# Attention maximum over two key halves: formed by GpSimd as difference, positive part and sum, with constant rows of -1

## The chip, the cores and the metric

The kernel runs on one core of a Trainium2 chip. The metric is the device time of one execution in microseconds; for a kernel, the median over its runs.

## What is computed

The program computes two layers over an input of 2 x 2048 tokens of width 128: `x = x + s * g`, where `s` comes from one branch and `g = silu(...)` from another. The first layer's `s` is the part that the change touches. Its two attention blocks have 8 heads of width 8 each, which gives 16 heads for each of the two batch rows:

```
q = (xin @ wq.T + bq).reshape(b, s, H, DK)      # H = 8, DK = 8
k = (xin @ wk.T + bk).reshape(b, s, H, DK)
scores = einsum('bshd,bthd->bhst', q, k) * (1.0 / sqrt(DK))
a = softmax(scores, axis=-1)
o = einsum('bhst,bthd->bshd', a, v)
```

The softmax subtracts the largest score of each query before the exponential. Beside it stands a mixture of 32 experts (4 for each token, at most 640 tokens for each expert), and behind both a state-space scan with a second, per-sequence expert network.

## The kernel before, in words

The program is written engine by engine, with semaphores between the engines and a fixed order on each. The attention is cut into 32 **units** (`UNITS`, one head of one batch row each). A unit has 2048 queries and 2048 keys.

For each unit there are two passes of TensorE over the scores:

- The **maximum pass** has 32 chunks (`CHUNKS`). Chunk n takes 128 queries against one half of the keys, 1024 of them, as two bf16 matmuls into two PSUM banks (`max_scores`, L1950). VectorE reduces each 128 x 1024 chunk to one column of `mxp` (L897): `mxp[:, n // 2, n % 2]` holds the maximum over key half n % 2 of query tile n // 2. There are two pairs of banks, so TensorE may be two chunks ahead of VectorE (the wait on `mx_done` in `max_scores`).
- The **score pass** has 64 steps e (`EXPS`). Each is one 512-column matmul (L2063), whose result ScalarE turns into exponentials (L1312). Groups of four exponentials are multiplied with the values (`weigh`, L1966). Twice in a unit ScalarE also evacuates the accumulated output (`evac`, L1301).

TensorE interleaves them: after every second score step comes one maximum chunk of a later place. The chunks run ahead by somewhat more than half a unit, so that chunk 0 of a unit is issued at about step 13 of the unit before, chunk 16 at about step 45, and chunk 31 at about step 11 of the unit itself.

Once 16 chunks (half a unit, 8 query tiles) are reduced, the maximum travels this way:

1. VectorE, `negated` (L849 to L854): one `tensor_reduce` of the 128 x 8 x 2 block of `mxp` to 128 x 8 with `negate=True`, into `nmx[:, 0]`. On VectorE's queue it stands behind the first chunk of the next half. It waits also for `spl_ready`, that is until GpSimd is done with an earlier half.
2. GpSimd, `largest` (L1602 to L1610): it waits for `nmx_ready` and splits the number in three bf16 parts with four small instructions (L1607 to L1610, a `plink` wait on the engine's own semaphore between them), into `spl`.
3. SyncE, `load_max` (L532 to L541): a DMA transpose of `spl` into `mT` (L537), and then two DMAs (L541) that put the three parts as rows into the query stacks `QS`. They raise `m_ld`.
4. TensorE's score pass waits for `m_ld` at steps 0 and 32 of each unit (L2060). The key stacks `KS` have constant rows at the same place. They are set once by GpSimd (L1578) and copied to the other stacks by SyncE; with rows of 1 in the keys and the negated maximum in the queries, the matmul L2063 yields score minus maximum.

The maximum pass uses 48 rows of the stacks (`MAXROWS`), the score pass 51, so that only the latter sees the constant rows.

GpSimd does other work in its fixed order between the calls of `largest`. In the first units it makes the routing tables of the experts (`plain` with `rows_step`). In the units called 12 to 19 there (`scatter`) it issues 16 indirect DMAs a unit (L1629), each released by one `pv_done` of TensorE; `largest(u - 3, 1)` stands ahead of the fourth and `largest(u - 2, 0)` ahead of the twelfth. Because of the offset of three, these run while TensorE is in the score pass of units 9 to 16. After the expert stage (785 to 910 us, in which no chunk is in work) it issues 12 indirect gathers a unit (`gather`, L1659), with `largest(u - 3, 1)` ahead of the fourth and `largest(u - 2, 0)` behind the last, followed by a `combine` of the unit before (L1637 to L1646). These run beside the score pass of units 18 to 28.

Of the kernel before, what the change touches and what calls it, by code (L numbers as in the profile page):

```python
# [6 lines left out]
ALU = mybir.AluOpType  # L7
# [3 lines left out]
X_AX = mybir.AxisListType.X  # L11
# [10 lines left out]
UNITS = G * B  # L22
# [9 lines left out]
TCH = S // P  # L32
STEPS = 2 * TCH
DFF = 512
CHUNKS = 2 * TCH
# [85 lines left out]
def after(eng, sem, count):  # L121

    if not isinstance(count, int) or count > 0:
        eng.wait_ge(sem, count)


def build(nc, a, out):
# [3 lines left out]
    with ExitStack() as ctx:  # L131
        def sb(name, shape, dt=F32):
            return ctx.enter_context(nc.sbuf_tensor(name, shape, dt))

        def sem(name):
            return ctx.enter_context(nc.semaphore(name))

        def dram(name, shape, dt=F32):
# [67 lines left out]
        KS = [stacks[:, (4 + i) * S:(5 + i) * S] for i in range(4)]  # L206
# [85 lines left out]
        mxp = sb("mxp", [P, TCH, 2])  # L292
        nmx = sb("nmx", [P, 2, TCH])
# [18 lines left out]
        ones_set = sem("ones_set")  # L312
# [16 lines left out]
        vh_ready, mxs_ready, mx_done, spl_ready, mt_ld = (  # L329
            sem(n) for n in ("vh_ready", "mxs_ready", "mx_done", "spl_ready", "mt_ld"))  # L330
# [12 lines left out]
        nmx_ready = sem("nmx_ready")  # L343
# [405 lines left out]
        def _(v):  # L749
# [72 lines left out]
            for d in range(1, NG):  # L822
                first, second = slice(0, NG - d), slice(d, NG)
# [22 lines left out]
            ins.then_inc(part2k, 1)  # L846


            def negated(uu, half):  # L849
                tiles = slice(TCH // 2 * half, TCH // 2 * (half + 1))  # L850
                v.wait_ge(mx_done, CHUNKS * uu + CHUNKS // 2 * (half + 1))
                after(v, spl_ready, 2 * uu + half - 1)
                v.tensor_reduce(nmx[:, 0, tiles], mxp[:, tiles, :], X_AX, ALU.max, negate=True).then_inc(nmx_ready, 1)  # L853

            def expert_h(e, w):
                v.wait_ge(sg_done, e + 1)
                v.wait_ge(mh_ready, 2 * e + 2)
                after(v, mo_ready, e - 1)
                halves = lambda t: t.rearrange("p (h c) -> p h c", h=2)
                v.tensor_tensor(halves(hhe[w % 2]), halves(sge[w % 2]), PS[:, 4:6, 0:CAP // 2], ALU.mult).then_inc(hh_done, 1)  # L860

            def expert_out(e, w, uses):
                v.wait_ge(mo_ready, e + 1)
                after(v, oes_st[w % 2], 16 * uses)
                v.tensor_copy(oe_s[w % 2][:, 0:512], PS[:, 6, :])
                v.tensor_copy(oe_s[w % 2][:, 512:CAP], PTF[:, 0:CAP - 512]).then_inc(oe_out, 1)  # L866
# [14 lines left out]
            def expert_stage():  # L881
                for e in range(E):
                    expert_h(e, e % 4)
                    if e > 0:
                        expert_out(e - 1, (e - 1) % 4, (e - 1) // 2)
                    if 0 <= e - NB - 2 < 4:
                        sums_inverse(0, e - NB - 2)
                    if e == NB + 6:
                        sum_weights()
                expert_out(E - 1, 3, E // 2 - 1)  # L890

            for uu in range(UNITS):
                for n in range(CHUNKS):
                    if CHUNKS * uu + n == CHUNK_AT:
                        expert_stage()
                    v.wait_ge(mxs_ready, CHUNKS * uu + n + 1)
                    v.tensor_reduce(mxp[:, n // 2, n % 2:n % 2 + 1], MXB[n % 2].rearrange("p a c -> p (a c)"), X_AX, ALU.max).then_inc(mx_done, 1)  # L897
                    if n == 0 and uu > 0:
                        negated(uu - 1, 1)
                    if n == CHUNKS // 2:  # L900
                        negated(uu, 0)
            negated(UNITS - 1, 1)


            v.wait_ge(c_ld, 16 * NLATE)
# [22 lines left out]
            half = lambda j: lambda t: PS[:, RES_BANK[j], t * DH:(t + 1) * DH]  # L928
# [192 lines left out]
            with v.If(v.value_load(flag[:, :], min_val=0, max_val=1) > 0):  # L1121
# [20 lines left out]
                for half in range(2):  # L1142
                    v.wait_ge(g_st, 16 * B * S // GT + 32 + 16 * half)
                    tiles = slice(NT // 2 * half, NT // 2 * (half + 1))
# [429 lines left out]
        def _(pool):  # L1574
            for i in range(4):
                pool.memset(VH[i][:, :, :], 1.0).then_inc(ones_set, 1)
            pool.wait_ge(ones_set, 4)
            pool.memset(KS[0][32:64, :], 1.0).then_inc(ones_set, 1)  # L1578
            pool.wait_ge(ones_set, 5)
            pool.memset(zt[:, :], 0.0).then_inc(ones_set, 1)  # L1580
            pool.wait_ge(ones_set, 6)
# [18 lines left out]
            plink = Chain(pool, pool_chain).link  # L1600

            def largest(uu, half):  # L1602
                tiles = slice(TCH // 2 * half, TCH // 2 * (half + 1))
                first, second = nmx[:, 0, tiles], nmx[:, 1, tiles]
                pool.wait_ge(nmx_ready, 2 * uu + half + 1)
                after(pool, mt_ld, 16 * (2 * uu + half - 1))
                plink(pool.tensor_copy(spl[:, half, 0, :], first))  # L1607
                plink(pool.tensor_tensor(second, first, spl[:, half, 0, :], ALU.subtract))
                plink(pool.tensor_copy(spl[:, half, 1, :], second))
                pool.tensor_tensor(spl[:, half, 2, :], second, spl[:, half, 1, :], ALU.subtract).then_inc(spl_ready, 1)  # L1610
# [840 lines left out]
```

## Time and profile before

| what | value |
|---|---|
| median of 3 runs | 1840.53 us (1836.5 to 1842.19) |
| the profiled execution | 1841.78 us |
| its span in the profile | 1839.7 us |
| mean granted TensorE clock | 0.974 of full speed |
| PE busy | 1711.9 us, 93% of the span |
| DVE (VectorE) busy | 1617.7 us, 88% |
| ACT (ScalarE) busy | 1477.5 us, 80% |
| POOL (GpSimd) busy | 654.0 us, 36% |
| HBM traffic | 74 GB/s over the span |

The span is what the profiler sees between the first and the last instruction; the execution's own time is 2.1 us more, and its time lies 1.25 us above the median of the runs. Busy times are shares of one engine's span and do not add up. Instructions of one engine may overlap in the records: the next one can start some tens of nanoseconds before the last one's end, so the time from start to start, not the mean duration, tells an engine's rate. The attention runs from about 77 us to 1432 us, with the expert stage in its middle.

### The profile page before, as it was taken

Reading aid. Unit: us, or ns where it says so; the run is one execution under the profiler, and the core shown is the slowest. Engines: PE = TensorE matmul, PEld = TensorE weight load, DVE = VectorE, ACT = ScalarE, POOL = GpSimd, SP = SyncE. Lnnn points to the kernel's source line nnn. Section 1 sums busy time; section 2 is a strip of 40 time slices with the busy share of each in tenths; the row PEclk is TensorE's granted clock in tenths of the full one; section 3 lists DMA queues with packets and bytes.
Section 4 is the critical chain, followed back from the end, with each engine's and each line's share of the span. In section 5 each row is a group of like instructions: output and inputs, shape, how many; then the busy total and the mean of one; then the engine's idle time right before and its main releaser. Section 6 shows DMA issues by size and latency. Waiting matters only on the chain.

```text
span 1839.7 us, 40114 instructions
## 1 busy us (share of the span) xinstructions
PE 1711.9 (93%) x15395; PEld 667.3 (36%) x15396; DVE 1617.7 (88%) x2338; ACT 1477.5 (80%) x2809; POOL 654.0 (36%) x932
## 2 busy tenths in 40 slices
PE   6799999999999999999999999999999699799784
PEld 4332222222222222278622222222222244366553
DVE  7799999999999999945599999999996677599778
ACT  5569999999999998943499999999999557777455
POOL 1423210232444444100045655566401233133447
PEclk9899999999999999999999999999999899899897
DMA  4422122111221122278412111211103233422121
GB/s 125 164 74 87 58 85 68 62 55 36 66 66 55 57 62 65 74 207 227 137 50 64 53 48 49 64 54 47 38 11 81 80 117 92 130 70 54 38 73 46
DMA packets 151357, 142.15 MB, mean 77 GB/s; under 512 B 38986, under 2 KB 130125, under 8 KB 151010
## 3 DMA queue, kind: packets, MB, share of 16 engines
q1 hardware_dynamic: 142818, 122.36, 22.6%
q0 software_dynamic: 8352, 17.29, 3.3%
q8 instruction: 118, 1.93, 0.5%
q14 instruction: 69, 0.57, 0.1%
HBM read 76.60 MB, written 60.03 MB: 74 GB/s over the span
## 4 chain that ended last, share of the span: by engine, by line
PE 72%; DVE 12%; ACT 9%; issue 4%; DMA 1%; POOL 1%; SPq 0%; DVEq 0%; ACTq 0%; POOLq 0%
PE PS L1966 28%; PE PS L2063 18%; PE PS L1950 10%; ACT probs L1312 7%; PE PS L2013 4%; PE PS L1998 2%; DVE hst L1084 1%; DVE VP L1061 1%; PE PS L1990 1%; PE PS L2176 1%; PE PS L2319 1%; DVE waq L919 1%; PE PS L2113 1%; DVE VP L1069 1%; DVE MXV L1090 1%
## 5 line engine op out<-in xcount | busy, mean ns | idle before, releaser
L897 DVE TENSOR_REDUCE mxp<-PS 128x1 f32<-128x1024 f32 x1024 | 1172.7, 1217 | 30.0 <-PE PS L1950 25.4
L1312 ACT ACTIVATE probs<-PS 128x512 f32<-128x512 f32 x2048 | 1096.2, 597 | 71.0 <-PE PS L2063 27.4
L1966 PE MATMUL PS<-probs,VH 128*32 128x256 f32 x8192 | 642.5, 391 | 2.3 <-ACT probs L1312 1.0
L2063 PE MATMUL PS<-stacks 51*128 51x512 bf16 x2048 | 444.0, 388 | 22.7 <-ACT probs L1312 18.7
L1950 PE MATMUL PS<-stacks 48*128 48x512 bf16 x2048 | 418.3, 381 | 9.6 <-DMA stacks<-qkl_d 8.5
L1966 PEld LDWEIGHTS PS<-probs,VH 128*32 128x32 f32 x8192 | 173.0, 108 | 400.1 <-issue 220.3
L2063 PEld LDWEIGHTS PS<-stacks 51*128 51x128 bf16 x2048 | 116.2, 93 | 463.7 <-ACT probs L1312 380.6
L1659 POOL DMA_INDIRECT S<-oe_d,ROWI x128 | 130.2, 1017 | 132.5 <-PE PS L1966 125.3
L1629 POOL DMA_INDIRECT xe_d<-S,ROWI x128 | 125.1, 977 | 140.1 <-PE PS L1966 118.0
L1607 POOL CAST spl<-nmx 128x8 bf16<-128x8 f32 x64 | 12.7, 199 | 305.7 <-DVE nmx L853 227.5
L1950 PEld LDWEIGHTS PS<-stacks 48*128 48x128 bf16 x2048 | 105.3, 95 | 34.0 <-DVE mxp L897 12.3
L1615 POOL TENSOR_TENSOR VH<-VP,bvb 128x128 f32<-128x128 f32 x32 | 14.4, 451 | 233.3 <-DMA oe_d<-XNT 138.3
L860 DVE TENSOR_TENSOR probs<-probs,PS 128x640 f32<-128x640 f32 x32 | 26.3, 821 | 58.0 <-ACT probs L1346 52.2
L2013 PE MATMUL PS<-probs,ews 128*128 128x320 f32 x256 | 74.3, 433 | 0.2 <-ACT probs L1346 0.2
L1337 ACT ACTIVATE probs<-PS 128x640 f32<-128x640 f32 x32 | 22.6, 705 | 61.4 <-PE PS L1990 61.3
L1810 POOL TENSOR_TENSOR stacks<-stacks,VH 128x512 f32<-128x512 f32 x16 | 24.9, 1555 | 92.7 <-ACT stacks L1497 92.7
L2013 PEld LDWEIGHTS PS<-probs,ews 128*128 128x128 f32 x256 | 46.1, 190 | 15.6 <-issue 0.4
L1998 PEld LDWEIGHTS PS<-ews,probs 128*128 128x128 f32 x320 | 40.7, 192 | 6.1 <-issue 1.2
L1998 PE MATMUL PS<-ews,probs 128*128 128x128 f32 x320 | 41.0, 275 | 1.1 <-DVE XNT L866 1.1
L1301 ACT ACTIVATE SG<-PS 128x512 f32<-128x512 f32 x64 | 37.9, 592 | 2.4 <-PE PS L1966 2.4
L1481 ACT ACTIVATE VP<-PS 128x1024 f32<-128x1024 f32 x16 | 16.4, 1025 | 26.2 <-PE PS L2243 24.7
L2176 PE MATMUL PS<-stacks,probs 128*128 128x512 f32 x64 | 33.4, 648 | 2.7 <-ACT SG L1413 2.7
(360 smaller groups left out, 1863.7 us busy)
## 6 DMA issues: line engine op xcount, KB each, us to landing
stacks<-qkl_d SPq DMA_DIRECT2D x128, 96.0 KB
xe_d<-zt SPq DMA_DIRECT2D x16, 640.0 KB
XNT<-xe_d SPq DMA_DIRECT2D x32, 320.0 KB, 3.8
oe_d<-XNT SPq DMA_DIRECT2D x32, 320.0 KB, 3.2
stacks<-qkl_d SPq DMA_DIRECT2D x128, 64.0 KB
o_d<-SG SPq DMA_DIRECT2D x256, 32.0 KB
ews<-in_ew_dram SPq DMA_DIRECT2D x33, 192.0 KB, 2.4
stacks<-qkl_d SPq DMA_DIRECT2D x128, 32.0 KB
```

Of the source, the lines that this page charges most:

```text
L860: v.tensor_tensor(halves(hhe[w % 2]), halves(sge[w % 2]), PS[:, 4:6, 0:CAP // 2], ALU.mult).then_inc(hh_done, 1)
L897: v.tensor_reduce(mxp[:, n // 2, n % 2:n % 2 + 1], MXB[n % 2].rearrange("p a c -> p (a c)"), X_AX, ALU.max).then_inc(mx_done, 1)
L1301: act.activation(OE[half][:, :], OB, ACT.Copy).then_inc(o_evac, 1)
L1312: act.activation(probs[:, at:at + 512], PS[:, bank_of(u, e), :], ACT.Exp, scale=float(1.0 / np.sqrt(np.float32(DK)))).then_inc(exp_done, 1)
L1629: pool.indirect_dma_start(xe_d, bass.IndirectOffsetOnAxis(ROWI[:, t, n:n + 1], 0), S0[:, t, :], None, bounds_check=E * CAP - 1, oob_is_err ...
L1659: pool.indirect_dma_start(GB[:, t % (2 * TB), n, :], None, oe_d, bass.IndirectOffsetOnAxis(ROWI[:, t, n:n + 1], 0), bounds_check=last_row, ...
L1950: mm = pe.matmul(MXB[n % 2][:, i, :], QS[w][o:o + MAXROWS, (n // 2) * P:(n // 2 + 1) * P], KS[w][o:o + MAXROWS, key:key + 512], start=True ...
L1966: mm = pe.matmul(OB[32 * jg:32 * jg + 32, c:c + 256], VH[w][:, kt, :], probs[:, at:at + 256], start=(kt < 2 and half == 0), stop=(kt >= TC ...
L1998: mm = pe.matmul(o, hhe[w % 2][:, t * P:(t + 1) * P], EW[w][:, 2, :], start=True, stop=True)
L2013: mm = pe.matmul(PS[:, 2 + 2 * m + h, 0:CAP // 2], EW[w][:, m, :], xeT[w % 2][:, h * CAP // 2:(h + 1) * CAP // 2], start=True, stop=True)
L2063: pe.matmul(PS[:, bank_of(u, e), :], KS[w][o:o + KROWS + 3, kt * P:(kt + 1) * P], QS[w][o:o + KROWS + 3, q0:q0 + 512], start=True, stop=Tr ...
L2176: pe.matmul(PS[:, 5 - t % 2, :], PJ[j][:, cols(t)], win[:, 0:2 * DI], start=True, stop=True).then_inc(zx_ready, 1)
```

## The change

On VectorE the function `negated` goes, with its 64 calls. The wait on `spl_ready` that stood in it moves to the first chunk of each half: VectorE may not overwrite half of `mxp` before GpSimd has read the earlier unit's values there. On GpSimd, `largest` waits for the 16 chunks themselves (`mx_done`) and forms the maximum of the two key halves a and b as `a + max(b - a, 0)`, with three instructions ahead of its four. The result is no longer negated, and the constant rows of the keys become -1 in its place. The order on TensorE, ScalarE and SyncE stays as it was.

```diff
@@ VectorE
-            def negated(uu, half):
-                tiles = slice(TCH // 2 * half, TCH // 2 * (half + 1))
-                v.wait_ge(mx_done, CHUNKS * uu + CHUNKS // 2 * (half + 1))
-                after(v, spl_ready, 2 * uu + half - 1)
-                v.tensor_reduce(nmx[:, 0, tiles], mxp[:, tiles, :], X_AX, ALU.max, negate=True).then_inc(nmx_ready, 1)
...
                 for n in range(CHUNKS):
                     if CHUNKS * uu + n == CHUNK_AT:
                         expert_stage()
+                    if n % (CHUNKS // 2) == 0:
+                        after(v, spl_ready, 2 * uu + n // (CHUNKS // 2) - 1)
                     v.wait_ge(mxs_ready, CHUNKS * uu + n + 1)
                     v.tensor_reduce(mxp[:, n // 2, n % 2:n % 2 + 1], MXB[n % 2].rearrange("p a c -> p (a c)"), X_AX, ALU.max).then_inc(mx_done, 1)
-                    if n == 0 and uu > 0:
-                        negated(uu - 1, 1)
-                    if n == CHUNKS // 2:
-                        negated(uu, 0)
-            negated(UNITS - 1, 1)
@@ GpSimd
-            pool.memset(KS[0][32:64, :], 1.0).then_inc(ones_set, 1)
+            pool.memset(KS[0][32:64, :], -1.0).then_inc(ones_set, 1)
...
             def largest(uu, half):
                 tiles = slice(TCH // 2 * half, TCH // 2 * (half + 1))
                 first, second = nmx[:, 0, tiles], nmx[:, 1, tiles]
-                pool.wait_ge(nmx_ready, 2 * uu + half + 1)
+                of_keys = [mxp[:, tiles, i] for i in range(2)]
+                pool.wait_ge(mx_done, CHUNKS * uu + CHUNKS // 2 * (half + 1))
+                plink(pool.tensor_tensor(second, of_keys[1], of_keys[0], ALU.subtract))
+                plink(pool.tensor_scalar(second, second, 0.0, None, ALU.max))
+                plink(pool.tensor_tensor(first, of_keys[0], second, ALU.add))
                 after(pool, mt_ld, 16 * (2 * uu + half - 1))
                 plink(pool.tensor_copy(spl[:, half, 0, :], first))
```

GpSimd's queue at the first unit of the scatter stage, before (L1629 is an indirect DMA, the bracket names the semaphores that a row waits for):

```order
L1629 DMA xe_d<-S,ROWI 20480x128
L1629 DMA xe_d<-S,ROWI 20480x128 [waits pv_done] x2
L1607 CAST spl<-nmx 128x8 [waits mt_ld,nmx_ready,pv_done]
L1608 TENSOR_TENSOR nmx<-nmx,spl 128x8 [waits pool_chain]
L1609 CAST spl<-nmx 128x8 [waits pool_chain]
L1610 TENSOR_TENSOR spl<-nmx,spl 128x8 [waits pool_chain]
L1629 DMA xe_d<-S,ROWI 20480x128
L1629 DMA xe_d<-S,ROWI 20480x128 [waits pv_done] x7
```

The same place in the changed kernel (lines 1598 to 1605 are its `largest`, line 1624 the indirect DMA):

```order
L1624 DMA xe_d<-S,ROWI 20480x128
L1624 DMA xe_d<-S,ROWI 20480x128 [waits pv_done] x2
L1598 TENSOR_TENSOR nmx<-mxp 128x8 [waits mx_done,pv_done]
L1599 TENSOR_SCALAR nmx<-nmx 128x8 [waits pool_chain]
L1600 TENSOR_TENSOR nmx<-mxp,nmx 128x8 [waits pool_chain]
L1602 CAST spl<-nmx 128x8 [waits mt_ld,pool_chain]
L1603 TENSOR_TENSOR nmx<-nmx,spl 128x8 [waits pool_chain]
L1604 CAST spl<-nmx 128x8 [waits pool_chain]
L1605 TENSOR_TENSOR spl<-nmx,spl 128x8 [waits pool_chain]
L1624 DMA xe_d<-S,ROWI 20480x128
L1624 DMA xe_d<-S,ROWI 20480x128 [waits pv_done] x7
```

Three instructions, each waiting for the one before, now stand between the third and the fourth indirect DMA, and the wait for `nmx_ready` has become one for `mx_done`.

VectorE's queue at the start of the maximum pass, before:

```order
L897 TENSOR_REDUCE mxp<-PS 128x1 [waits mxs_ready] x17
L853 TENSOR_REDUCE nmx<-mxp 128x8 [waits mx_done]
L897 TENSOR_REDUCE mxp<-PS 128x1 [waits mxs_ready] x16
L853 TENSOR_REDUCE nmx<-mxp 128x8 [waits mx_done]
L897 TENSOR_REDUCE mxp<-PS 128x1 [waits mxs_ready] x16
L853 TENSOR_REDUCE nmx<-mxp 128x8 [waits spl_ready,mx_done]
```

and in the changed kernel (line 893 is the reduction of a chunk):

```order
L893 TENSOR_REDUCE mxp<-PS 128x1 [waits mxs_ready] x32
L893 TENSOR_REDUCE mxp<-PS 128x1 [waits mxs_ready,spl_ready]
L893 TENSOR_REDUCE mxp<-PS 128x1 [waits mxs_ready] x15
L893 TENSOR_REDUCE mxp<-PS 128x1 [waits mxs_ready,spl_ready]
L893 TENSOR_REDUCE mxp<-PS 128x1 [waits mxs_ready] x15
```

The small reductions are gone, and from the second unit on every 16th chunk has a second semaphore to wait for.

## Rows read from the trace of the kernel before

**Rows 1.** The page: busy us, share of the span and instructions of each engine.

```profile
PE 1711.9 (93%) x15395; PEld 667.3 (36%) x15396; DVE 1617.7 (88%) x2338; ACT 1477.5 (80%) x2809; POOL 654.0 (36%) x932
```

**Rows 2.** Groups by line: names, shapes, count | busy us, mean ns | idle us before, releaser.

```profile
L897 DVE TENSOR_REDUCE mxp<-PS 128x1 f32<-128x1024 f32 x1024 | 1172.7, 1217 | 30.0 <-PE PS L1950 25.4
L1608 POOL TENSOR_TENSOR nmx<-nmx,spl 128x8 f32<-128x8 f32 x64 | 13.2, 206 | 5.4
L1714 POOL TENSOR_SCALAR gs<-gs 128x32 f32<-128x32 f32 x1 | 0.3, 299 | 0.1
```

**Rows 3.** Waits over the whole span: us in total, times, longest us.

```profile
POOL spl L1607 <- DVE nmx L853: 227.5, 22, 19.4
...
PEld PS L1950 <- DVE mxp L897: 12.3, 21, 1.0
```

**Rows 4.** Windows, one unit each: length, then busy of PE, PEld, DVE, ACT, POOL.

```profile
372.72:409.45 36.73, 36.22 (x389) 9.58 (x386) 36.54 (x35) 35.06 (x67) 12.69 (x21) 1.00 0.22 69
...
594.64:631.60 36.96, 36.34 (x389) 10.66 (x386) 36.54 (x35) 35.17 (x67) 17.61 (x25) 1.00 0.20 61
...
1170.61:1207.48 36.87, 36.36 (x388) 9.65 (x385) 36.63 (x35) 34.98 (x67) 21.89 (x33) 1.00 0.20 54
```

**Rows 5.** Timeline of PE in unit 7: start us, length us, line.

```profile
378.72 0.39 PE L2063 MATMUL PS<-stacks 51*128 51x512 bf16 x2
...
383.18 0.41 PE L2063 MATMUL PS<-stacks 51*128 51x512 bf16 x2
```

**Rows 6.** Timeline of DVE in unit 8, merged runs of one line.

```profile
416.14 2.35 DVE L897 TENSOR_REDUCE mxp<-PS 128x1 f32<-128x1024 f32 x2
418.40 0.16 DVE L853 TENSOR_REDUCE nmx<-mxp 128x8 f32<-128x16 f32 x1
418.47 14.89 DVE L897 TENSOR_REDUCE mxp<-PS 128x1 f32<-128x1024 f32 x13
433.67 1.23 DVE L897 TENSOR_REDUCE mxp<-PS 128x1 f32<-128x1024 f32 x1 [0.30 <-PE PS L1950]
...
439.41 11.39 DVE L897 TENSOR_REDUCE mxp<-PS 128x1 f32<-128x1024 f32 x10
```

**Rows 7.** Timeline of POOL in unit 9 (scatter stage).

```profile
455.99 0.19 POOL L1607 CAST spl<-nmx 128x8 bf16<-128x8 f32 x1 [0.56 <-PE PS L1966]
456.27 0.20 POOL L1608 TENSOR_TENSOR nmx<-nmx,spl 128x8 f32<-128x8 f32 x1
...
457.50 1.02 POOL L1629 DMA_INDIRECT xe_d<-S,ROWI  x1 [0.50 <-issue]
458.94 0.97 POOL L1629 DMA_INDIRECT xe_d<-S,ROWI  x1 [0.42 <-issue]
461.18 0.97 POOL L1629 DMA_INDIRECT xe_d<-S,ROWI  x1 [1.27 <-PE PS L1966]
```

**Rows 8.** Timeline of DVE at the same place.

```profile
455.50 4.61 DVE L897 TENSOR_REDUCE mxp<-PS 128x1 f32<-128x1024 f32 x4
460.32 3.49 DVE L897 TENSOR_REDUCE mxp<-PS 128x1 f32<-128x1024 f32 x3 [0.21 <-PE PS L1950]
```

**Rows 9.** Timeline in unit 16, three indirect DMAs in a row: POOL's last, DVE behind it.

```profile
721.86 0.98 POOL L1629 DMA_INDIRECT xe_d<-S,ROWI  x1 [0.55 <-issue]
...
723.70 2.44 DVE L897 TENSOR_REDUCE mxp<-PS 128x1 f32<-128x1024 f32 x2 [0.57 <-PE PS L1950]
```

**Rows 10.** Timeline of POOL at the start of unit 26 (gather stage).

```profile
1209.90 0.46 POOL L1615 TENSOR_TENSOR VH<-VP,bvb 128x128 f32<-128x128 f32 x1 [1.08 <-PE PS L1966]
```

**Rows 11.** Timeline of SP and PE at the start of units 2 and 26.

```profile
184.09 1.54 SPq L541 DMA_DIRECT2D stacks<-mT  x2
...
186.88 0.39 PE L2063 MATMUL PS<-stacks 51*128 51x512 bf16 x2 [0.84 <-DMA stacks<-mT]
...
1203.31 1.56 SPq L541 DMA_DIRECT2D stacks<-mT  x2
...
1207.48 0.39 PE L2063 MATMUL PS<-stacks 51*128 51x512 bf16 x2
```

## The prediction

> **What bounds the kernel now.** The change touches the attention alone, so I asked who paces a unit there. The page [rows 1] does not say: TensorE, VectorE and ScalarE are all busy for 80% or more of the span, and GpSimd for 36%. Next I read the groups by line. VectorE's chunk reductions are the costliest group of the program, 1172.7 us for 1024, with only 30.0 us of idle time ahead of them [rows 2]. That looks as if VectorE paced everything, and then each instruction taken off it would count in full. Three further views speak against it.
>
> First, the waits: TensorE's maximum matmuls waited for a VectorE reduction 21 times of 1024, 12.3 us in all [rows 3]. If VectorE were the bound, TensorE would stand before its buffers in nearly every cycle.
>
> Second, the timelines. In a quiet stretch one cycle of TensorE (two score steps, one maximum chunk, one group of values) takes (383.18 - 378.72) / 4 = 1.115 us [rows 5]. VectorE needs, from start to start, (11.39 - 1.22) / 9 = 1.13 us for a chunk [rows 6], where 1.22 is the length of one reduction. So VectorE is the slower of the two by 0.015 us a chunk and falls behind a little. Then, twice a unit, ScalarE evacuates the output. TensorE loses time there, and VectorE, which has caught up, waits for it (0.30 us ahead of the reduction at 433.67, [rows 6]). The lag starts again from nothing.
>
> Third, the sum of a unit. VectorE's own work is 32 x 1.13 = 36.16 us plus two small reductions. The small one lasts 0.16 us, but overlaps its neighbours: the second chunk of the run at 416.14 starts at 417.27, the next would be due at 418.40, and it starts at 418.47 [rows 6]. It costs 0.07 us of the queue. So VectorE needs 36.16 + 0.14 = 36.30 us, and the unit takes 36.73 [rows 4]. The remaining 0.43 us is waiting for TensorE (the window shows less idle time, 36.73 - 36.54 = 0.19, because each record runs on some 0.1 us past the point at which the next could start). **In a quiet unit the loop of TensorE and ScalarE sets the pace, and VectorE has 0.43 us to spare.**
>
> The units of the scatter stage differ. Unit 13 takes 36.96 us [rows 4]. There GpSimd issues indirect DMAs, each released by TensorE, and `largest` delays the next one, so that two follow closely: 457.50 and 458.94, with 0.42 us between the end of one and the start of the other [rows 7]. Behind such a pair VectorE is late: four reductions from 455.50 make the next due at 455.50 + 4 x 1.13 = 460.02, and it starts at 460.32, 0.30 us late [rows 8]. The timeline shows one such pair and one such delay in each of the 16 halves of units 9 to 16. With two of 0.30, VectorE needs 36.30 + 0.60 = 36.90 us: in these eight units it is VectorE that paces.
>
> **Part 1: the small reduction goes.** It frees 64 x 0.07 = 4.5 us of VectorE's queue. What of it reaches the end is read by stage. In quiet units and in the gather stage (unit 25 takes 36.87 us with VectorE idle for 0.24, [rows 4]) VectorE only waits 0.14 us longer for TensorE, and nothing is won. In the eight scatter units 0.14 us each can be won before TensorE's 36.73 stands in the way: -1.1 us. Before the score pass begins, one more small reduction lies in the run-up: -0.1 us. Together -1.2 us.
>
> **Part 2: three instructions more on GpSimd.** The nearest row is a 128x8 subtraction, 206 ns, and the starts of two linked ones lie 456.27 - 455.99 = 0.28 us apart [rows 2, 7]. The positive part is a tensor_scalar, for which the nearest row is a larger one, 128x32, at 299 ns [rows 2]; I count it like the others, and 0.1 us more as the upper end. Three links make 0.84 us a call, 54 us over 64 calls. GpSimd is idle for about two thirds of the span [rows 1], so the work itself is covered. The lateness is what counts. The Trainium skill (GPSIMD Engine Reference, Engine selection) advises against moving elementwise work to this engine and calls it about twice as slow for two inputs; by that, three times twice 0.16 us would be 0.96 us, which would change the sum by less than 0.2 us a call.
>
> **Part 3: the wait.** `largest` no longer waits for the small reduction, which stood behind one more chunk. Where GpSimd had waited for it (22 calls, [rows 3]), it can start 1.13 + 0.14 = 1.3 us sooner and is done about 0.4 us sooner. In the scatter and gather stages it stands behind `pv_done` or an indirect DMA and not behind the reduction, so there it ends 0.84 us later. Next in the chain are SyncE's transpose and loads. In the gather stage the load for the first half of unit 26 leaves SyncE at 1203.31 + 1.56 = 1204.87, and the matmul that needs it starts at 1207.48: 2.61 us. How short that may get is shown at unit 2, the one place where TensorE did wait for this load: 185.63 to 186.88, 1.25 us [rows 11]. So 1.36 us of cover is left, of which the change takes 0.84. Cost 0. Without the cover each half would pay what is missing. GpSimd's next `values` waited 1.08 us for TensorE in the gather stage [rows 10], which also covers 0.84.
>
> **Part 4: the moved wait on `spl_ready`.** VectorE now asks, before chunk 0 of a unit, whether GpSimd is done with the first half of the unit before. But this chunk is issued at step 13 of that earlier unit, whose score pass could only start once those maxima were loaded. The same holds for the second halves. The wait is always met: 0. The fill with -1 and its copies cost what they did with 1: 0.
>
> **Part 5: closer indirect DMAs.** With `largest` 0.84 us longer, the DMA at 457.50 moves to about 458.3 and ends at 459.3. The one behind it starts 0.42 later at 459.7 and ends at 460.7. The third, at 461.18 [rows 7], then follows by 0.5 us and not by 1.27. Each half of a scatter unit gets a second close pair. No row shows what a second one costs. The lower end is 0 (the pair costs nothing if the delay belongs to the first alone), and the upper end is unit 16, where three followed closely and the reduction behind the third waited 0.57 us [rows 9]. The nearest in kind is the first pair's 0.30 us; but the gap is a little wider, so I take 0.2 us: 16 x 0.2 = +3.2 us, all on the path, since VectorE paces there. The range of this term is 0 to 9.1 us. In the gather stage the same happens once a unit (11 units), but there VectorE has its idle time as cover: 0, and 11 x 0.57 = 6.3 us without it.
>
> **The sum** is -1.2 + 3.2 = +2.0 us: 1843.8 for the profiled execution of 1841.78, and 1842.5 against the median of 1840.53, since that execution lies 1.25 above the median. A measurement of this kernel can tell about 0.3%, 5.5 us, from no change. The forecast is a change too small to be told.
>
> **Rivals.**
> - *Close pairs don't touch VectorE.* Then the late reductions have another cause, parts 1 to 4 alone count, and the time is 1840.5 - 1.2 = 1839.3. For it: the reduction reads PSUM and writes one column. Against it: sixteen delays of sixteen. The Trainium skill (SBUF — State Buffer, Who interferes with whom) says that a tensor_reduce never contends with GpSimd on this chip; by that rule this rival would hold. The delayed start at 460.32 is no proof against the rule, since that row doesn't name the cause, but it makes me give this case 0.2.
> - *VectorE paces all units*, so that the small reductions are worth their place everywhere: 1840.5 - 4.5 = 1836.0, or with their whole length of 0.16 us 64 x 0.16 = 10.2, 1830.3. Against it stand the 21 waits [rows 3]. Chance 0.08.
> - *Slower: the second close pair costs as in unit 16.* The place is the fourth to sixth indirect DMA of each half in the scatter stage, and of each unit in the gather stage. The price is 0.57 us, 27 times: 15.4 - 1.2 = +14.2, 1854.7. Speaking for it: in unit 16 it did just that [rows 9]. It turns to slower by over 0.3% once a pair costs (5.5 + 1.2) / 27 = 0.25 us on the path. Chance 0.16.
> - *The loads come late*: if the chain grows by more than 1.36 us and not by 0.84 (a cold tensor_scalar, or a longer landing). At 1.7 us, 11 units would pay 0.34 each: +3.7 on top of the forecast, 1846.2. Chance 0.04.
>
> My own case has the remaining 0.52. Faster by over 0.3% (below 1835.0) needs the second rival with more than its 0.07 us, or scatter of the runs: 0.05. Slower by over 0.3% (above 1846.0) is the third rival and the upper part of my term for the pairs: 0.18. The rest is 0.77. The range runs from 1836.0, the second rival's near end, to 1850.0, my sum with the pairs at their upper end less part of the gather stage; about 0.07 is left out on either side.
>
> **What would show it.** In the changed profile a quiet unit should still take 36.73 us, with more idle time ahead of VectorE's reductions (about 0.14 us a unit more). GpSimd's seven instructions should end about 1.9 us after the first one's start in place of 1.0. In unit 9 the third indirect DMA behind `largest` should follow the second by about 0.5 us, and a late reduction should stand behind it. Units 9 to 16 together should be longer by some 2 us. I am wrong if quiet units get shorter by 0.1 us or more, if TensorE waits for the load of the maxima in units 18 to 28, or if VectorE shows a wait for GpSimd at a first chunk.

## The result, and the profile after

| | before | after |
|---|---|---|
| median | 1841.36 us (6 runs, 1836.5 to 1844.31) | 1854.22 us (6 runs, 1853.49 to 1857.77) |
| span of the profiled execution | 1839.7 us | 1851.7 us |
| ratio after / before | | 1.0079, 95% interval 1.0069 to 1.0089 |

The change makes the kernel slower by 12.9 us between the medians, and by 0.8% by the ratio. I had forecast 1842.5 us and a range up to 1850.0, so the result lies outside. The time of my third rival, 1854.7, was met to half a microsecond, though not quite for its reasons.

The page of the changed kernel, busy us by engine, answers to [rows 1]:

```profile
PE 1718.9 (93%) x15395; PEld 660.3 (36%) x15396; DVE 1613.4 (87%) x2274; ACT 1475.6 (80%) x2809; POOL 697.0 (38%) x1124
```

VectorE lost 4.3 us of busy time and GpSimd gained 43.0 with 192 instructions. No engine's share says where 12 us went. The windows do. First the kernel before: the eight units of the scatter stage (9 to 16) and ten units of the gather stage (19 to 28). The columns are those of [rows 4], whose first row is the quiet unit 7.

```profile
446.47:745.02 298.55, 292.40 (x3076) 82.75 (x3072) 293.26 (x272) 280.90 (x529) 140.23 (x199) 1.00 0.20 62
948.68:1318.98 370.30, 364.93 (x3845) 97.36 (x3842) 366.31 (x341) 349.79 (x661) 215.07 (x327) 1.00 0.19 53
```

Unit 7 and the same two stretches of the changed kernel, each again from the first score matmul of one unit to that of another:

```profile
370.79:407.52 36.73, 36.22 (x388) 9.59 (x386) 36.45 (x33) 35.05 (x67) 14.00 (x27) 1.00 0.21 68
444.54:755.04 310.50, 299.95 (x3076) 79.32 (x3073) 294.60 (x257) 279.81 (x529) 151.93 (x247) 1.00 0.19 59
960.36:1333.62 373.26, 366.15 (x3844) 96.71 (x3841) 366.09 (x321) 349.78 (x661) 228.53 (x387) 1.00 0.19 53
```

The quiet unit takes the same 36.73 us, with 0.09 us more idle time on VectorE (I had expected about 0.14). The scatter units together take 11.95 us more, and the gather units 2.96 us. The granted clock is 1.00 in all of them. What else differs between the two profiles (the score pass starts 2.0 us sooner, unit 18 takes 1.7 us more, the part from the start of unit 31 on is 2.7 us shorter) changes by as much between kernels that are alike there: over the runs of this study the start lay between 107.7 and 111.9 us, unit 18 took 39.1 to 40.9 us, and the end part 444.6 to 447.3 us. I leave it out of the account.

GpSimd in unit 9 of the changed kernel, timeline, answers to [rows 7]:

```profile
454.08 0.20 POOL L1598 TENSOR_TENSOR nmx<-mxp 128x8 f32<-128x8 f32 x1 [0.58 <-PE PS L1961]
454.36 0.24 POOL L1599 TENSOR_SCALAR nmx<-nmx 128x8 f32<-128x8 f32 x1
...
455.77 0.20 POOL L1605 TENSOR_TENSOR spl<-nmx,spl 128x8 bf16<-128x8 f32 x1
456.48 1.10 POOL L1624 DMA_INDIRECT xe_d<-S,ROWI  x1 [0.51 <-PE PS L1961]
457.88 0.97 POOL L1624 DMA_INDIRECT xe_d<-S,ROWI  x1 [0.30 <-issue]
459.34 0.97 POOL L1624 DMA_INDIRECT xe_d<-S,ROWI  x1 [0.49 <-issue]
462.02 0.97 POOL L1624 DMA_INDIRECT xe_d<-S,ROWI  x1 [1.71 <-PE PS L1961]
```

`largest` now lasts 1.89 us (454.08 to 455.97) where it had lasted 1.01. Behind it three indirect DMAs follow each other with gaps of 0.30 and 0.49 us; before, it was one gap of 0.42 and then 1.27. VectorE at the same place, answers to [rows 8]:

```profile
454.64 4.60 DVE L893 TENSOR_REDUCE mxp<-PS 128x1 f32<-128x1024 f32 x4
459.40 1.23 DVE L893 TENSOR_REDUCE mxp<-PS 128x1 f32<-128x1024 f32 x1 [0.16 <-PE PS L1945]
461.09 2.44 DVE L893 TENSOR_REDUCE mxp<-PS 128x1 f32<-128x1024 f32 x2 [0.46 <-PE PS L1945]
```

It starts late twice: 459.40 where 454.64 + 4 x 1.13 = 459.16 was due, and 461.09 where 460.53 was due. This is more than VectorE's matter, as ScalarE and TensorE show. ScalarE's timeline there:

```profile
454.87 3.88 ACT L1303 ACTIVATE probs<-PS 128x512 f32<-128x512 f32 x7
459.39 1.09 ACT L1303 ACTIVATE probs<-PS 128x512 f32<-128x512 f32 x2 [0.64 <-PE PS L2058]
461.01 2.06 ACT L1303 ACTIVATE probs<-PS 128x512 f32<-128x512 f32 x4 [0.54 <-PE PS L2058]
```

and TensorE's (L2058 are score steps, L1945 a maximum chunk):

```profile
458.37 0.39 PE L2058 MATMUL PS<-stacks 51*128 51x512 bf16 x2
458.60 0.38 PE L1945 MATMUL PS<-stacks 48*128 48x512 bf16 x2
458.91 0.64 PE L1961 MATMUL PS<-probs,VH 128*32 128x256 f32 x8
459.48 0.39 PE L2058 MATMUL PS<-stacks 51*128 51x512 bf16 x1
460.04 0.39 PE L2058 MATMUL PS<-stacks 51*128 51x512 bf16 x1 [0.17 <-issue]
```

The score matmuls of 458.37 are in the records done by 458.76. The exponential that takes their result starts at 459.39, although ScalarE had been idle for 0.64 us. The semaphore records kept in the trace agree: the update that announces this matmul stands at 459.30, 0.54 us behind its modelled end, where those of unit 7 stand at most 0.05 us behind. TensorE in turn gets its next pair apart, at 459.48 and 460.04. The signal the other way is not late here: the exponential of 459.39 ends at 459.98, and the matmul of 460.04 follows 0.06 us later. So behind the close DMAs ScalarE and VectorE start on TensorE's results 0.4 to 0.6 us late, and since TensorE and ScalarE feed each other, both lose it. That is the loop that paces the unit.

Set cycle by cycle against the quiet unit, TensorE of the changed kernel loses 1.0 to 1.1 us behind the three close DMAs of each half of units 9 to 15 (0.5 in the second half of unit 14). In the kernel before, it lost less than 0.05 us behind the pair of the first half of these units. Behind that of the second half it lost 0.25 us or less in units 9, 10, 12 and 13, and 0.7 to 0.8 us in units 11, 14 and 15, although the gap was 0.41 to 0.43 us each time. The gap alone does not set the price. Here are TensorE's score matmuls of the kernel before in unit 9, at the place of [rows 8]:

```profile
459.18 0.41 PE L2063 MATMUL PS<-stacks 51*128 51x512 bf16 x2
460.31 0.39 PE L2063 MATMUL PS<-stacks 51*128 51x512 bf16 x2
461.42 0.41 PE L2063 MATMUL PS<-stacks 51*128 51x512 bf16 x2
```

The cycles last 1.13 and 1.11 us, as they do in the quiet unit. VectorE's delay of 0.30 us at 460.32, which the prediction built on, cost TensorE nothing there.

In the gather stage one event stands out. At the start of unit 28 TensorE waits for the load of the maxima (timelines of TensorE, then of SyncE, in the changed kernel):

```profile
1294.31 0.41 PE L2058 MATMUL PS<-stacks 51*128 51x512 bf16 x2
...
1296.50 0.39 PE L2058 MATMUL PS<-stacks 51*128 51x512 bf16 x2 [0.99 <-DMA stacks<-mT]
```

```profile
1289.86 1.13 SPq L537 DMA_TRANSPOSE mT<-spl  x1
1293.70 1.55 SPq L541 DMA_DIRECT2D stacks<-mT  x2
```

and SyncE at the same place in the kernel before:

```profile
1275.62 1.15 SPq L537 DMA_TRANSPOSE mT<-spl  x1
1277.93 1.55 SPq L541 DMA_DIRECT2D stacks<-mT  x2
```

The loads follow the transpose after 3.84 us instead of 2.31, and the step takes 2.19 us instead of 1.115: 1.07 of the 2.96 us. In the nine units before, all first-half loads follow after 2.28 to 2.30 us, and TensorE does not wait.

Most of the other 1.9 us stand behind close DMAs again: behind `largest` two now stand 0.30 us apart in the gather stage too (1269.13 and 1270.54 in GpSimd's timeline), where before it was 1.12 (1255.22 and 1257.38), and TensorE loses 0.36 to 0.41 us there in each of the ten units. It had lost 0.13 to 0.18 us at about this place before, in most units with no gap under 1.1 us by then, so close spacing is not the only cause of such losses.

The longest single delay behind a close pair in the gather stage is hardly the change's: TensorE's cycle from 1276.24 is 0.82 us longer than a quiet one, behind a GpSimd pause of 2.34 us and another close pair, and the kernel before has the same pause (2.07 us), the same pair (0.30) and a cycle 0.72 us longer. Its ScalarE waited there:

```profile
1262.90 3.44 ACT L1312 ACTIVATE probs<-PS 128x512 f32<-128x512 f32 x6 [0.57 <-PE PS L2063]
```

The removal of the small reduction gave nothing in a quiet unit, where its cost was no part of the loop: four of TensorE's cycles there take (381.26 - 376.80) / 4 = 1.115 us each in its timeline, as in [rows 5].

### The profile page after: what moved, and what is told of

It reads as the page before. It is cut to its first block, busy times and chain, and to the rows that moved or that the text cites. A ratio compares the mean times of both kernels' runs of the same rounds, so it can differ in the third digit from the quotient of the medians.

```text
span 1851.7 us, 40274 instructions
## 1 busy us (share of the span) xinstructions
PE 1718.9 (93%) x15395; PEld 660.3 (36%) x15396; DVE 1613.4 (87%) x2274; ACT 1475.6 (80%) x2809; POOL 697.0 (38%) x1124
## 4 chain that ended last, share of the span: by engine, by line
PE 70%; DVE 13%; ACT 9%; issue 3%; POOL 2%; DMA 2%; SPq 0%; POOLq 0%; DVEq 0%; ACTq 0%
PE PS L1961 28%; PE PS L2058 18%; PE PS L1945 10%; ACT probs L1303 7%; PE PS L2008 4%; PE PS L1993 2%; DVE hst L1075 1%; DVE waq L910 1%; PE PS L1985 1%; DVE VP L1052 1%; DVE VP L1060 1%; DVE mxp L893 1%; PE PS L2314 1%; PE PS L2171 1%; DVE MXV L1081 1%
## 5 line engine op out<-in xcount | busy, mean ns | idle before, releaser
L2058 PE MATMUL PS<-stacks 51*128 51x512 bf16 x2048 | 454.4, 388 | 28.1 <-ACT probs L1303 21.1
L1945 PE MATMUL PS<-stacks 48*128 48x512 bf16 x2048 | 426.2, 381 | 9.9 <-DMA stacks<-qkl_d 8.7
L2058 PEld LDWEIGHTS PS<-stacks 51*128 51x128 bf16 x2048 | 117.8, 93 | 480.5 <-ACT probs L1303 389.4
L1598 POOL TENSOR_TENSOR nmx<-mxp 128x8 f32<-128x8 f32 x64 | 13.2, 206 | 281.2 <-DVE mxp L893 260.9
L1945 PEld LDWEIGHTS PS<-stacks 48*128 48x128 bf16 x2048 | 106.0, 95 | 26.0 <-DVE mxp L893 13.4
```

The costliest lines, as they stand in the source:

```text
L1945: mm = pe.matmul(MXB[n % 2][:, i, :], QS[w][o:o + MAXROWS, (n // 2) * P:(n // 2 + 1) * P], KS[w][o:o + MAXROWS, key:key + 512], start=True ...
L2058: pe.matmul(PS[:, bank_of(u, e), :], KS[w][o:o + KROWS + 3, kt * P:(kt + 1) * P], QS[w][o:o + KROWS + 3, q0:q0 + 512], start=True, stop=Tr ...
```

## The experiments

Theory A: the longer `largest` pushes GpSimd's indirect DMAs together, and closely spaced indirect DMAs hold up the other engines. The rivals: B, VectorE's side (the moved wait) costs the time; C, the length of `largest` itself does, by later loads; D, the stall needs a DMA of SyncE at the same time; E, any busy GpSimd would do it. Five of the kernels were timed once. The argument goes by the windows, from one profile for each kernel.

### VectorE's side alone

```diff
-                plink(pool.tensor_tensor(second, of_keys[1], of_keys[0], ALU.subtract))
-                plink(pool.tensor_scalar(second, second, 0.0, None, ALU.max))
-                plink(pool.tensor_tensor(first, of_keys[0], second, ALU.add))
                 after(pool, mt_ld, 16 * (2 * uu + half - 1))
-                plink(pool.tensor_copy(spl[:, half, 0, :], first))
-                plink(pool.tensor_tensor(second, first, spl[:, half, 0, :], ALU.subtract))
+                plink(pool.tensor_copy(spl[:, half, 0, :], of_keys[0]))
+                plink(pool.tensor_tensor(second, of_keys[0], spl[:, half, 0, :], ALU.subtract))
```

> VectorE's side of the change alone: the small reduction is gone and the wait on spl_ready stands at the first chunk of each half, but GpSimd has its old four instructions; it splits the maximum over the first key half only, so the maximum over the second half is left out. Theory A (GpSimd's longer largest pushes indirect DMAs together, and the signals between the engines come late behind them): scatter units 9 to 16 as before or 0.1 us shorter each, about 1840 us. Theory B (the moved wait or the missing wait behind one chunk costs the time): about 1854 us, with units 9 to 16 at 38.8 us.

Measured: 1841.9 us, ratio 0.9999 (0.999 to 1.0009). Its units 9 to 16, window:

```profile
444.48:741.73 297.25, 291.85 (x3077) 83.55 (x3074) 291.75 (x256) 280.94 (x529) 140.22 (x199) 1.00 0.20 63
```

That is 1.3 us less than before's 298.55, and nothing in the quiet and gather units (36.73 and 370.54). B falls. The 1.3 us are too few to show in the total. They are not spread as 0.14 us a unit either: units 14 and 15 take 36.83 and 36.95 us where they had taken 37.44 and 37.41, which is 1.1 of the 1.3 us, and units 9, 10, 11 and 16 stay within 0.03 us.

### GpSimd's side alone

```diff
                 pool.wait_ge(nmx_ready, 2 * uu + half + 1)
+                plink(pool.tensor_tensor(second, first, first, ALU.subtract))
+                plink(pool.tensor_scalar(second, second, 0.0, None, ALU.max))
+                plink(pool.tensor_tensor(second, first, second, ALU.add))
                 after(pool, mt_ld, 16 * (2 * uu + half - 1))
```

> GpSimd's side alone: the kernel before with three linked 128x8 instructions more at the head of largest, whose results are not used; VectorE as before. Theory A: 1852 to 1857 us, units 9 to 16 at about 38.8 us, plain units at 36.73 us. Theory B (VectorE's side): within 3 us of the kernel before.

Measured: 1859.63 us, ratio 1.0103 (1.0085 to 1.0121), units 9 to 16:

```profile
448.44:760.84 312.40, 301.83 (x3076) 78.75 (x3074) 297.11 (x273) 279.75 (x529) 151.64 (x247) 0.99 0.19 60
```

Three instructions whose results nobody uses cost 18 us. That is 3 us more than I expected at most. 13.9 us of it are in the scatter stage, with the 38.8 us in most units and 41.85 us in unit 16; 3.0 us are in the gather stage. Unit 18 (40.72 us, 1.5 more) and the stretch ahead of the score pass (it starts at 111.9 us, 2.0 later) add to them, and the part from unit 31 on takes 2.3 us away; these places vary from kernel to kernel.

### Without the close followers

```diff
+                        if step in (4, 12):
+                            continue
                         pool.indirect_dma_start(xe_d, bass.IndirectOffsetOnAxis(ROWI[:, t, n:n + 1], 0), S0[:, t, :], None,
...
-            pool.wait_ge(sc_st, 64 * NT)
+            pool.wait_ge(sc_st, 64 * NT - 256)
```

The same edit was made in the changed kernel (skip_4_12) and in the kernel before (before_skip_4_12).

> The changed kernel without the indirect DMAs of steps 4 and 12 of each scatter unit (16 of 128, that part of the scatter is left out), so that the DMA behind largest has no close follower, while GpSimd's arithmetic stays as long. Theory A: units 9 to 16 fall from 38.8 to 36.7 to 36.9 us, the total to about 1841 us, with the gather stage's 3 to 4 us still in it. Theory C (the length of largest itself, that is the later loads of the maxima, costs the time): units 9 to 16 stay near 38.8 us, 1853 us.

> The kernel before without the indirect DMAs of steps 4 and 12 of each scatter unit (that part of the scatter is left out). Beside skip_4_12 it is the change without close gaps in the scatter stage. Theory A: units 9 to 16 together at 294 to 294.6 us, the same as with the change (294.4). If GpSimd's arithmetic, the later loads or the missing reduction counted in themselves, the two would differ by 1 us or more.

Measured: 1840.13 us for the changed kernel without those DMAs (ratio to the kernel before 0.9992, 0.9979 to 1.0004), and 1838.22 us in one run for the kernel before without them. Units 9 to 16 of skip_4_12:

```profile
446.21:740.64 294.43, 290.27 (x3076) 77.96 (x3072) 291.74 (x257) 279.99 (x529) 136.31 (x231) 1.00 0.19 59
```

and of before_skip_4_12:

```profile
447.27:741.36 294.09, 289.94 (x3078) 76.70 (x3074) 292.30 (x273) 280.28 (x529) 124.87 (x183) 1.00 0.19 60
```

With the DMA spacing made safe, the changed and the unchanged kernel differ by 0.3 us over eight units, and both run at 36.7 to 36.8 us a unit (37.0 and 37.1 in unit 16). C falls for the scatter stage: there the longer `largest` and the later loads cost nothing. In the gather stage, where the edit takes no DMA away, the changed kernel stays 2.9 us slower (373.28 against 370.35 us), and one late load is part of it, again at unit 28 (1.18 us of waiting). The kernel before pays too: without its close pairs units 9 to 16 take 298.55 - 294.09 = 4.5 us less. Of these 2.9 us are in units 9 to 15. The 1.6 us of unit 16 also hold a burst of DMAs that moved out of this stage with the count (see the last section).

### GpSimd kept busy, but not with a DMA

```diff
                         if step in (4, 12):
+                            plink(pool.tensor_tensor(zt[:, :], zt[:, :], zt[:, :], ALU.add))
                             continue
```

> As skip_4_12 (the changed kernel without DMAs 4 and 12 of each scatter unit, left out), but with a GpSimd addition over 128x256 elements, some 0.7 us long, in the place of each DMA left out. Theory A (it is the indirect DMA's own work, not GpSimd's being busy): units 9 to 16 stay near 36.8 us. Theory E (any busy GpSimd instruction there delays the other engines): units go to 37.5 us or more.

Measured: 1838.92 us in one run, with the additions at 0.66 us each, units 9 to 16:

```profile
446.75:741.17 294.42, 290.27 (x3077) 77.99 (x3074) 291.66 (x257) 279.99 (x529) 146.93 (x247) 1.00 0.19 59
```

To 0.01 us the same as skip_4_12, with 146.93 - 136.31 = 10.6 us more of GpSimd's busy time. E falls for such an addition: it takes an indirect DMA. Whether its issue on GpSimd or its transfer does it, this does not tell.

### Close DMAs elsewhere

In the base without DMAs 4 and 12 a chain of linked 128x8 copies delays one other DMA, so that it meets its followers. Here for step 7 with seven copies; triple_at_7 has eleven, pair_at_9 has eight ahead of step 9.

```diff
+                        if step == 7:
+                            for _ in range(7):
+                                plink(pool.tensor_copy(nmx[:, 1, 0:TCH // 2], nmx[:, 1, 0:TCH // 2]))
                         pool.indirect_dma_start(xe_d, bass.IndirectOffsetOnAxis(ROWI[:, t, n:n + 1], 0), S0[:, t, :], None,
```

> As before_skip_4_12, but with seven linked dummy instructions on GpSimd ahead of the DMA of step 7 of each scatter unit, far from the transposes and loads of the maxima, so that DMAs 7, 8 and 9 follow closely. Theory A (close spacing alone is enough): each of units 9 to 16 gets 0.7 to 1.1 us longer than 36.75, near step 30 to 40 of the unit. Theory D (the stall needs SyncE's load of the maxima at the same time): units stay at 36.75.

> As before_skip_4_12, but with eight linked dummy instructions ahead of the DMA of step 9 of each scatter unit, where SyncE issues nothing in the second half of the wait (its loads of the next unit and its stores are done). DMAs 9 and 10 then follow closely. Theory A (spacing alone): a pair costs 0.2 to 0.5 us, units 9 to 16 together at 296 to 298 us beside 294.1. Theory D (a DMA of SyncE must be issued at the same time): 294 to 294.6.

> As chain_at_7, with eleven linked dummy instructions in place of seven, so that the DMAs of steps 7, 8 and 9 follow each other with gaps of about 0.3 us. In chain_at_7 the one close pair cost 0.37 us a unit. Theory A1 (the delay grows faster than the number of close followers, as the changed kernel's 1.0 us for each three suggests): 0.9 to 1.2 us a unit, units 9 to 16 together at 301.3 to 303.7 us. Theory A2 (each close gap costs the same): 0.7 to 0.8 us a unit, about 300 us.

GpSimd's timeline in unit 10 of chain_at_7, one gap of 0.30:

```profile
503.17 0.98 POOL L1634 DMA_INDIRECT xe_d<-S,ROWI  x1 [1.08 <-PE PS L1971]
504.45 0.98 POOL L1634 DMA_INDIRECT xe_d<-S,ROWI  x1 [0.30 <-issue]
506.80 0.97 POOL L1634 DMA_INDIRECT xe_d<-S,ROWI  x1 [1.37 <-PE PS L1971]
```

and of triple_at_7, gaps of 0.30 and 0.56:

```profile
505.74 0.98 POOL L1634 DMA_INDIRECT xe_d<-S,ROWI  x1 [0.78 <-POOL nmx L1633]
507.03 0.97 POOL L1634 DMA_INDIRECT xe_d<-S,ROWI  x1 [0.30 <-issue]
508.56 0.97 POOL L1634 DMA_INDIRECT xe_d<-S,ROWI  x1 [0.56 <-issue]
```

The single times are 1839.29 us for chain_at_7, 1839.48 for pair_at_9 and 1847.58 for triple_at_7. The windows of units 9 to 16 in the same order:

```profile
444.91:741.97 297.06, 292.39 (x3078) 77.23 (x3074) 293.06 (x273) 279.73 (x529) 135.83 (x239) 1.00 0.19 59
```

```profile
447.69:743.00 295.31, 291.18 (x3076) 82.84 (x3072) 291.95 (x272) 280.27 (x529) 136.95 (x247) 1.00 0.19 59
```

```profile
445.57:751.43 305.86, 295.70 (x3077) 77.76 (x3074) 293.82 (x273) 280.59 (x529) 141.76 (x271) 1.00 0.19 57
```

Over the base of 294.09 us that is 2.97, 1.22 and 11.77 us, or 0.37, 0.15 and 1.47 us a unit. (In chain_at_7 I had expected three in a row and 0.7 to 1.1 us; only two came close.) Two things follow. The stall goes wherever the close DMAs go, far from the transposes and the loads of the maxima. And three in a row cost four times what two do. That is A1's direction, and beyond its upper end of 1.2 us.

D falls in its strict form. In triple_at_7 SyncE's last store was out at 507.59, ahead of the third DMA (508.56), and most of the loss comes behind that one. SyncE's and TensorE's timelines:

```profile
505.89 1.70 SPq L529 DMA_DIRECT2D o_d<-SG  x4
```

```profile
509.68 0.39 PE L2068 MATMUL PS<-stacks 51*128 51x512 bf16 x1
510.72 0.39 PE L2068 MATMUL PS<-stacks 51*128 51x512 bf16 x1 [0.66 <-ACT probs L1312]
511.83 0.39 PE L2068 MATMUL PS<-stacks 51*128 51x512 bf16 x2
```

This cycle takes 511.83 - 509.68 = 2.15 us, 1.04 more than a quiet one, with SyncE issuing nothing (its stores' transfers may still have been under way). A part of D stays open. In pair_at_9 SyncE also issued nothing while the pair ran, and the pair cost 0.15 us, less than the 0.2 I had expected at least. In chain_at_7 SyncE issued output stores just then, and the pair cost 0.37. Other DMA traffic may thus add to the stall, but the place in TensorE's cycle differs as well. The runs don't tell the two apart.

### `largest` ahead of the wait

```diff
-                        if step:
-                            pool.wait_ge(pv_done, TCH * (u - 3) + step)
                         if step == 3:
                             largest(u - 3, 1)
                         if step == 11:
                             largest(u - 2, 0)
+                        if step:
+                            pool.wait_ge(pv_done, TCH * (u - 3) + step)
```

The same in `gather` for step 3. early_largest is the changed kernel with it, before_early the kernel before.

> The changed kernel with largest placed ahead of the wait for pv_done of its step, not behind it, in scatter and gather stage. It can then start some 0.5 us sooner, the fourth DMA goes out sooner, and one of the two close gaps opens. Theory A: at least half of the loss comes back, 1841 to 1848 us, units 9 to 16 at 37 to 37.8 us. Theory B or C (VectorE's side, or arithmetic on GpSimd as such): stays at 1852 or more.

> The kernel before (VectorE's small reduction, four instructions on GpSimd) with largest ahead of its step's wait for pv_done in scatter and gather stage. Theory A (closely spaced indirect DMAs cost the time, wherever they come from): the one close gap of 0.42 us of each half widens to 0.6 us or more, units 9 to 16 together fall from 298.6 to about 295 us, and the whole to about 1837 us, below both kernels. Theory C (the pairs of the kernel before cost nothing and its scatter units have another cause): within 1 us of the kernel before.

Measured: early_largest 1843.63 us, ratio 1.0016 (1.0003 to 1.0029); before_early 1837.62 us, ratio 0.9982 (0.9971 to 0.9994). GpSimd's timeline in unit 9 of before_early:

```profile
456.20 1.02 POOL L1629 DMA_INDIRECT xe_d<-S,ROWI  x1 [0.50 <-issue]
457.99 0.97 POOL L1629 DMA_INDIRECT xe_d<-S,ROWI  x1 [0.77 <-PE PS L1966]
460.23 0.97 POOL L1629 DMA_INDIRECT xe_d<-S,ROWI  x1 [1.27 <-PE PS L1966]
```

and its windows of units 9 to 16 and 19 to 28:

```profile
445.51:741.34 295.83, 290.43 (x3076) 77.04 (x3072) 292.57 (x273) 280.21 (x529) 140.44 (x199) 1.00 0.20 63
946.40:1315.06 368.66, 362.82 (x3846) 96.33 (x3842) 365.74 (x341) 350.37 (x661) 215.02 (x327) 1.00 0.19 53
```

No work is left out here. The gap of 0.42 us has become 0.77, and units 9, 10 and 12 to 15 now take exactly the quiet unit's 36.73 us. The gather units gain 1.6 us. This kernel is the fastest of the study: 0.18% below the kernel before by the ratio, and 0.9% below the changed one (1837.62 / 1854.22, from different sets of runs). In the changed kernel the same edit takes back most of the loss of the total, but its `largest` is too long to avoid the pair: with gaps of 0.30 and about 1.25 us, units 9 to 15 take 37.35 to 37.50 us, some 0.35 us for each pair. Unit 16 takes 41.15 us, more than the 39.27 of the changed kernel, behind a longer burst (units 9 to 16 together: 303.2 us).

## Why the prediction was wrong

**What bounds the kernel: right for a quiet unit, wrong for the scatter stage.** The loop of TensorE and ScalarE paces a quiet unit. All runs have 36.73 us there, with or without the small reduction. In units 9 to 16 I had VectorE pace, from one unit's 36.96 us. But at the late reduction of [rows 8] TensorE's cycles went on at 1.13 and 1.11 us, and units 11, 14, 15 and 16 took 37.4 to 38.6 us in the kernel before, which a sum of 36.90 does not explain.

**Part 1, -1.2 us: right in size, by luck.** VectorE's side alone gave -1.3 us in the scatter units and nothing elsewhere. But I had 0.14 us in each of eight units; measured are 1.1 us in units 14 and 15 together, where a longer TensorE cycle behind the second pair became a short one. Why is open.

**Part 2: right in size.** I had 0.84 us for the three instructions and measured 1.89 - 1.01 = 0.88; the tensor_scalar lasts 0.24 us. The work itself is covered, as units 9 to 16 of skip_4_12 show.

**Part 3, 0: wrong once, by 1.07 us.** I had said that a wait of TensorE for the load in units 18 to 28 would speak against me, and at unit 28 it came. My cover of 1.36 us was real, and 0.84 fitted into it in the other ten units; but I had taken the time from the transpose to the loads as fixed, and there it was 1.5 us longer. All five kernels with the seven-instruction `largest` (after, gpsimd_side, skip_4_12, filler_4_12, early_largest) show this at unit 28, 3.78 to 4.17 us with 0.9 to 1.3 us of waiting; the other seven have 2.28 to 2.46 us there and no wait. Why the transpose is slow just there stays open.

**Part 4, 0: right.** VectorE showed no wait for GpSimd at a first chunk.

**Part 5: this step failed, in size and in kind.** I had named the right place and the right event: a second close gap behind each `largest`, 0.5 us wide (0.49 measured). My term was 16 x 0.2 = 3.2 us with an upper end of 16 x 0.57. Measured are 11.95 us net, or 13.2 us with the 1.3 of part 1 taken as won; GpSimd's side alone gave 13.85. That is 0.75 to 0.87 us for each half, beyond the upper end. Two readings led me there.
- I took the delay for one of VectorE's queue, because only there I had looked (460.32 in place of 460.02). The delay that costs is one of TensorE and ScalarE, that is of the loop without slack; in the second half of units 11, 14 and 15 the kernel before already showed it. For the same reason "VectorE's idle time covers it" was no argument in the gather stage: I had 0, and about 1.9 us came. Unit 13's 36.96 us, which I explained by VectorE's sum of 36.90, agreed by accident of size. In the kernel before, with VectorE's work unchanged, taking away the followers alone gave 36.73.
- I treated the cost as one sum for each gap. It grows faster: two DMAs in a row cost 0.37 us and three 1.47 at the same place. The row of unit 16 [rows 9], where three had followed closely, was the nearest to the new state, and not the first pair's 0.30 us from which I took my value. That unit took 38.58 us in the kernel before, and I had not asked why.

**The rival that came true** gave 14.2 us with 0.57 us for each of 27 gaps. The total came out nearly right by luck, the split did not: it is 0.75 to 0.87 in the scatter stage and about 0.2 in the gather stage, and a late load stands beside it. I had given this rival a chance of 0.16, and yet put its 1854.7 outside a range that was to leave only 0.07 above it; the two don't agree. The rival of the late loads (a longer landing) also came true, at one unit of its eleven; I had given it 0.04.

**The rule of the Trainium skill** (SBUF — State Buffer, Who interferes with whom), that a tensor_reduce never contends with GpSimd: the trace agrees with it. The reductions themselves last 1210 to 1227 ns after the change and 1212 to 1227 before. I had weighed it as a reason for a time of 1839.3 us; but a reduction can be untouched and still start late, because the matmul it waits for is announced late.

## What to carry to other kernels

When a loop without slack runs beside indirect DMAs issued by GpSimd, the spacing of these DMAs is a resource: three of them within 4 us cost 1 to 1.5 us of the loop's time here, and a little more arithmetic between them is enough to bunch them. Put work that is ready ahead of the wait that releases the next DMA, not behind it. And when one engine starts late without a reason of its own, look at the others in the same microsecond before you call their slack a cover.

## What the runs showed that I had not expected

Closely spaced indirect DMAs hold up engines that share no data with them. In unit 9 what comes late is the announcement of TensorE's matmuls. What makes it late (the semaphores, or the matmuls' real ends, which the profile only models) is not shown by these runs, and neither is why pairs with the same gap cost 0 at one place and 0.7 us at another.

GpSimd also pauses at the 114th indirect DMA of every kernel. In the kernel before, timeline of unit 16:

```profile
709.85 0.99 POOL L1629 DMA_INDIRECT xe_d<-S,ROWI  x1 [0.25 <-issue]
715.25 0.98 POOL L1629 DMA_INDIRECT xe_d<-S,ROWI  x1 [4.40 <-issue]
716.53 0.97 POOL L1629 DMA_INDIRECT xe_d<-S,ROWI  x1 [0.30 <-issue]
```

It sits idle for 4.40 us with nothing to wait for, then catches up with a burst, and unit 16 is the slowest of its stage. In the changed kernel the pause is 4.82 us, at the same count; over all kernels it is 4.40 to 5.27 us. In before_skip_4_12, which issues 16 DMAs fewer ahead of it, it is again the 114th, now at the start of the gather stage (4.91 us), and unit 16, now without the burst and without its close pairs, takes 37.00 us instead of 38.58. So it goes by the count and not by the place. What it is was not tried.
